# First attention: two accumulating transfers in place of two of TensorE's four sources of the denominators, with eight slots of probabilities

## The reference

```
cp = leaky_relu(x @ Wc.T + bc)                  # q, k: 16 heads x 8; v: 16 heads x 64
scores = einsum('bqhd,bkhd->bhqk', q, k) / SCALE
attn = softmax(scores, axis=-1)
out = einsum('bhqk,bkhd->bqhd', attn, v)
proj = leaky_relu(out @ Wo.T + bo)
```

## Time and profile before

| | us |
|---|---|
| median of the two runs | 1003.67 (1001.41 and 1005.93) |
| span of the profiled execution, first to last instruction | 1003.72 |
| first matmul of the denominators of unit 0, of unit 31 | 177.65, 612.77 |
| PE busy in the span | 920.3 (92%) |
| POOL busy in the span | 597.9 (60%) |

### The profile page before, as it was taken

The page is one execution under the profiler, slowest core; times in us unless marked ns, Lnnn a source line. Parts: engine busy times, 40 slices in busy tenths (PEclk is TensorE's granted clock), DMA queues, the critical chain, the costliest instruction groups (busy, mean ns, idle before and its releaser), DMA issues. The chain is left out here.

```text
span 1003.7 us, 20954 instructions
## 1 busy us (share of the span) xinstructions
PE 920.3 (92%) x7704; PEld 489.4 (49%) x7713; DVE 764.0 (76%) x1332; ACT 538.3 (54%) x901; POOL 597.9 (60%) x533
## 2 busy tenths in 40 slices
PE   5799997999999999999989997899889787799997
PEld 3346563233333333333323233798788444488794
DVE  6978888888888889887888825883689998873514
ACT  1255345666766666666756775443266243274463
POOL 3660425788778777887777893123735886652333
PEclk9999998999999999999999999799999997999999
DMA  9372525111111101111101123567651200243462
GB/s 319 137 225 88 153 64 156 41 51 46 26 52 28 58 24 49 34 55 56 35 26 44 40 67 116 161 193 241 225 156 35 89 22 22 79 142 101 143 196 79
DMA packets 92308, 97.17 MB, mean 97 GB/s; under 512 B 23184, under 2 KB 68624, under 8 KB 91952
## 3 DMA queue, kind: packets, MB, share of 16 engines
q1 hardware_dynamic: 87088, 85.34, 27.8%
q0 software_dynamic: 5120, 10.50, 3.6%
HBM read 70.57 MB, written 24.77 MB: 95 GB/s over the span
## 5 line engine op out<-in xcount | busy, mean ns | idle before, releaser
L255 PE MATMUL ps<-ar 64*64 64x512 bf16 (+5 forms) x5312 | 538.6, 448 | 17.7 <-ACT ar L301 4.3
L255 PEld LDWEIGHTS ps<-ar 64*64 64x64 bf16 (+2 forms) x5312 | 268.5, 137 | 273.4 <-ACT ar L301 92.0
L277 DVE TENSOR_REDUCE small<-ps 128x2 f32<-128x1024 f32 (+2 forms) x276 | 307.2, 1140 | 52.0 <-PE ps L255 50.6
L301 ACT ACTIVATE ar<-ps 128x1024 f32<-128x1024 f32 (+1 forms) x304 | 285.4, 941 | 113.1 <-PE ps L255 106.5
L264 POOL TENSOR_TENSOR psum_sb<-psum_sb,ar 128x1024 f32<-128x1024 f32 x91 | 214.8, 2360 | 57.3 <-DVE on_sb L264 47.1
L264 POOL TENSOR_TENSOR ar<-ar 128x512 f32<-128x512 f32 (+1 forms) x80 | 79.2, 995 | 52.1 <-DVE ar L277 30.0
L323 POOL DMA_INDIRECT gT<-ysort,rt x48 | 46.9, 977 | 98.7 <-issue 97.7
L264 DVE TENSOR_TENSOR ar<-ps,ar 128x256 f32<-128x256 f32 (+4 forms) x56 | 56.2, 1011 | 47.9 <-PE ps L255 43.4
L264 POOL TENSOR_TENSOR psum_sb<-ar 128x1024 f32<-128x1024 f32 x32 | 75.9, 2372 | 16.8 <-ACT ar L301 15.6
L298 ACT COPY ar<-ps 128x256 f32<-128x256 f32 (+1 forms) x84 | 31.8, 386 | 80.8 <-PE ps L255 50.2
L255 PE MATMUL ps<-wA,xnT 128*128 128x512 f32 (+3 forms) x192 | 62.0, 447 | 5.3 <-DVE ar L264 2.7
(11 more groups left out here) (156 smaller groups left out, 1066.0 us busy)
## 6 DMA issues: line engine op xcount, KB each, us to landing
ar<-in_L_up SPq DMA_DIRECT2D x48, 384.0 KB, 4.1
ar<-in_L_b SPq DMA_DIRECT2D x32, 322.0 KB, 3.4
rec_sb<-lscr SPq DMA_DIRECT2D x64, 128.0 KB
scr<-ar SPq DMA_DIRECT2D x48, 128.0 KB, 2.1
ar<-xsort SPq DMA_DIRECT2D x40, 128.0 KB
ysort<-ar SPq DMA_DIRECT2D x40, 128.0 KB, 3.3
ar<-scr SPq DMA_DIRECT2D x32, 112.0 KB
xsort<-xs SPq DMA_DIRECT2D x12, 256.0 KB, 6.2
```

What stands on the lines that cost most here:

```text
L255: return self.e.matmul(o, l, r, start=start, stop=stop) if self.e else Nothing()
L277: return self.e.tensor_reduce(o, a, AX.X, op, negate=True) if negate else self.e.tensor_reduce(o, a, AX.X, op)
L301: return self.e.activation(o, a, fn, **kw) if self.e else Nothing()
```

## The change

For the units with `u % 16 < 14` (`by_dma`, 28 of 32) POOL adds blocks 0 to 3 with three operations as before. Block 4 is added to that sum by an accumulating transfer that POOL issues at k = 6, and block 5 is added to block 6 in place by a second one at k = 7, issued after P times V of block 6 is done. At k = 1 of the next unit, behind that unit's first add, POOL waits for both transfers and adds block 6 (which now holds 5 and 6) to the sum. TensorE sums two sources, this sum and block 7, at k = 5 of the next unit (`SUM_STEP`) in place of k = 1. The steps of the reciprocal and of scaling move by four with it (k = 9, 10 and 14); the projection stays at k = 17 and takes a pair of banks of its own. There are eight slots, one for each block of a unit: two lie outside the old area (`ps2_sb`, and the new `p7_sb`). A slot's next `exp` waits for whatever reads it last (for block 5 the second transfer, for block 6 POOL's fourth add). POOL's wait for "scaled" is gone. `BY_DVE` goes from 27 to 30, so units 27 to 29 are done like the others; units 14, 15, 30 and 31 keep the four sources.

```diff
-BY_DVE = 27
-NP = 6
+BY_DVE = 30
+NP = 8
+SUM_STEP = 5
...
+    def dma_add(self, o, i):
+        return self.e.dma_start(o, i, accum_op=ALU.add) if self.e else Nothing()
...
+    p7_sb = sb("p7_sb", [128, 1024])
+    Ps = [area(POFF + 1024 * i, 1024) for i in range(6)] + [ps2_sb[:, :], p7_sb[:, :]]
...
+    def by_dma(u):
+        return u % 16 < 14
+    def sum_step(u):
+        return SUM_STEP if by_dma(u) else 1
...
-            if k == 1:
+            if k == sum_step(u) and by_dma(u):
+                b = island(u) + 1
+                pe.wait_ge(*at("exp", 8 * u + 7))
+                pe.wait_ge(*at("sums", u, 4))
+                for n, src in enumerate((Ps[7], psum_sb[:, 1024 * (u % 2):1024 * (u % 2) + 1024])):
+                    for a in range(2):
+                        r = 64 * n + 32 * a
+                        ins = pe.mm(ps[r:r + 32, b, :], onesf[:, 0:32], src[:, 512 * a:512 * a + 512])
+                ins.then_inc(*filled(b, ("sum", u)))
+            elif k == sum_step(u):
...
-                b = island(u + 2) if proj_step(u) == 17 else take(ring[0])
+                b = island(u + 2) if u % 16 in (12, 13) else take(ring[0])
...
+                    if by_dma(u) and k > 3:
+                        act.wait_ge(*(at("fourth_in", u), at("fifth_in", u), at("sums", u, 4), at("sum", u))[k - 4])
...
-                    if u >= BY_DVE:
-                        pool.wait_ge(*at("scaled", u - 2))
-                    pool.tt(a_, Ps[:, (i - 1) % NP, :], Ps[:, i % NP, :], ALU.add).then_inc(*up(("sums", u, 1)))
-                elif 2 <= k <= (4 if u < BY_DVE else 3):
-                    if k == 2 and 2 <= u < BY_DVE:
-                        pool.wait_ge(*at("scaled", u - 2))
+                    pool.tt(a_, Ps[0], Ps[1], ALU.add).then_inc(*up(("sums", u, 1)))
+                    if u and by_dma(u - 1):
+                        before = psum_sb[:, 1024 * ((u - 1) % 2):1024 * ((u - 1) % 2) + 1024]
+                        pool.wait_ge(*at("fourth_in", u - 1))
+                        pool.wait_ge(*at("fifth_in", u - 1))
+                        pool.tt(before, before, Ps[6], ALU.add).then_inc(*up(("sums", u - 1, 4)))
+                elif 2 <= k <= (3 if by_dma(u) or u >= BY_DVE else 4):
                     pool.wait_ge(*at("exp", i))
                     pool.wait_ge(*at("sums", u, k - 1))
-                    pool.tt(a_, a_, Ps[:, i % NP, :], ALU.add).then_inc(*up(("sums", u, k)))
+                    pool.tt(a_, a_, Ps[k], ALU.add).then_inc(*up(("sums", u, k)))
+                elif k == 6 and by_dma(u):
+                    pool.wait_ge(*at("exp", 8 * u + 4))
+                    pool.wait_ge(*at("sums", u, 3))
+                    pool.dma_add(a_, Ps[4]).then_inc(*landed(("fourth_in", u)))
+                elif k == 7 and by_dma(u):
+                    pool.wait_ge(*at("pvd", 8 * u + 6))
+                    pool.dma_add(Ps[6], Ps[5]).then_inc(*landed(("fifth_in", u)))
```

More of the change, by code:

```diff
@@ L509, in _program @@
     POFF = KOFF + 3 * 1024
-    assert POFF + NP * 1024 <= AR
+    assert POFF + 6 * 1024 <= AR
     V0 = area(0, 16384)
@@ L513, in _program @@
     Ks = area(KOFF, 3 * 1024).bitcast(BF16).rearrange("p (s h t) -> p s h t", s=3, h=2)
-    Ps = area(POFF, NP * 1024).rearrange("p (s t) -> p s t", s=NP)
     acc_sb = sb("acc_sb", [128, T])
@@ L789, in pv @@
                                 V0[r, 1024 * tile + 64 * h:1024 * tile + 64 * h + 64],
-                                Ps[r, i % NP, 512 * a:512 * a + 512], start=kt == 0, stop=kt == 7)
+                                Ps[i % NP][r, 512 * a:512 * a + 512], start=kt == 0, stop=kt == 7)
                 if kt == 7:
@@ L803, in unit_tail @@
                 pe.wait_ge(*(at("sums", u, 4) if u < BY_DVE else at("sums_dve", u)))
-                for n, src in enumerate((Ps[:, (8 * u + 5) % NP, :],
-                                         psum_sb[:, 1024 * (u % 2):1024 * (u % 2) + 1024],
-                                         Ps[:, (8 * u + 6) % NP, :], Ps[:, (8 * u + 7) % NP, :])):
+                for n, src in enumerate((Ps[5], psum_sb[:, 1024 * (u % 2):1024 * (u % 2) + 1024], Ps[6], Ps[7])):
                     for a in range(2):
@@ L1263, in unit_tail @@
                     *emptied(("pvd", 8 * u + 7), ("osb", u)))
-            if k == 5:
+            if k == sum_step(u) + 4:
                 dve.wait_ge(*at("lcol_in", u))
@@ L1270, in unit_tail @@
                 dve.rec(lsum, lsum).then_inc(*up(("lcol_dve", u)))
-            if k == 10:
+            if k == sum_step(u) + 9:
                 dve.wait_ge(*at(f"recip_in{m}", u))
@@ L1310, in attention @@
                     dve.wait_ge(*at("sums", u, 3))
-                    dve.tt(a_, a_, Ps[:, (8 * u + 4) % NP, :], ALU.add).then_inc(*up(("sums_dve", u)))
+                    dve.tt(a_, a_, Ps[4], ALU.add).then_inc(*up(("sums_dve", u)))
                 tails(i)
@@ L1858, in unit_tail @@
                     *emptied(("pvd_low", 8 * u + 7), ("osb_low", u)))
+            if k == sum_step(u):
                 act.wait_ge(*at("sum", u))
@@ L1878, in attention @@
                     k, u = (i - NP) % 8, (i - NP) // 8
-                    act.wait_ge(*(at("sum", u) if k > 4 else at("sums_dve", u) if k == 4 and u >= BY_DVE else
-                                  at("sums", u, max(k, 1))))
-                act.af(Ps[:, i % NP, :], ps[:, b0:b0 + 2, :].rearrange("p a t -> p (a t)"), ACT.Exp,
+                    if by_dma(u) and k > 3:
+                        act.wait_ge(*(at("fourth_in", u), at("fifth_in", u), at("sums", u, 4), at("sum", u))[k - 4])
+                    else:
+                        act.wait_ge(*(at("sum", u) if k > 4 else at("sums_dve", u) if k == 4 and u >= BY_DVE else
+                                      at("sums", u, max(k, 1))))
+                act.af(Ps[i % NP], ps[:, b0:b0 + 2, :].rearrange("p a t -> p (a t)"), ACT.Exp,
                        scale=SCALE).then_inc(*emptied(("st", i), ("exp", i)))
@@ L2367, in unit_tail @@
                 sp.dma(lcol[:, 8:16], lrow[64:128:32, :]).then_inc(*landed(("lcol_in", u)))
-            if k != 6:
+            if k != sum_step(u) + 5:
                 return
```

## The result

The changed kernel takes 1112.43 us (1111.48 to 1113.38) against 1003.67 us: a ratio of 1.108, interval 1.103 to 1.113. It is slower, as forecast, by 109 us where 58 were forecast; the time lies 2 us above the range.

A forecast was written before the change was run, and what follows sets the result against it. TensorE was taken to bound the attention before, POOL's turn after. To 1003.7 us came 39 us for turns 1.4 us longer in 28 units and 19 of side work: 1062 us, range 980 to 1110.

The forecast's parts named there:

- POOL's turn with a visible landing: POOL's queue per unit: two issues, W, three adds, 9.61 + W = 15.1 us against 13.71; chance 0.50, 1062 us.
- W: Time from the end of POOL's second issue to the landing, taken as 5.5 us, between 2.4 and 12.
- the second read and the queue: Half a microsecond added to the 5.0 us of a plain 512 KB transfer for reading the destination and queueing.
- The fourth rival: The second transfer waits for the first, two full reads each: landing 10.0 us, turn 19.6, 1188 us; chance 0.10.
- The lower end of my forecast: The forecast case by itself ran from 1025 us (landing after 4.1 us) to 1110 us (after 7.2 us).
- the lock: DVE's scaling stands still during a POOL add: 1.23 in place of 0.68 us in the one scaling that met one.
- the side work: POOL's gathers, scatters, normalisation and routing, 36 us from 200 to 600 us; half hidden, 19 us added to the time.
- Edits that I cost at nothing: Eight slots, moved steps, one more bank pair and units 27 to 29 were taken to add no time.
- the first rival: TensorE stays the bound, landing under 3.2 us: each unit gives 0.86 us, 980 us; chance 0.10.
- a floor: TensorE's two saved rounds, 0.86 us in 28 units, 24 us, all on the path: 1003.7 - 24 = 980 us.
- The third rival: Without POOL's wait for the scaled product, DVE's scaling meets POOL's adds and DVE becomes the bound: 1014 us; chance 0.08.
- its two signs: Signs that DVE had become the bound: DVE idle nowhere, and its scaling at 1.2 to 3 us.

The follow-up runs named there:

- the two-source run: The kernel before, with only TensorE's sum cut to the collected blocks and block 7 (blocks 5 and 6 left out of the denominators): 979.9 us, -21.

## Why the prediction was right, and where it was wrong

**The mechanism and the sign were right, and the sum was 50 us short.** POOL's turn with a visible landing sets the unit: POOL waits in nearly every unit, TensorE's sum waits up to 4.1 us for `psum_sb`, and taking the wait and its add away gives 78 of the 109 us back.

**The step that failed by size is W,** the time from the end of the second issue to its landing. I took 5.5 us; the landing of 7.6 less the issue of 1.10 makes 6.5, and 8.2 in the turn shown. The half microsecond for "the second read and the queue" was the error: plain copies in pairs land in 5.4 us, adding makes it 7.6, and alone an adding transfer takes 4.9. The Trainium skill ("Collectives: The Full Stack", section "The bandwidth ceiling: the fold count and why AG ≠ RS ≠ AR") has the two reads as the price of an add in the DMA engine, in collectives. The trace agrees that the add in flight has a price, 2.2 us for two transfers and 1.9 times the engines' time a megabyte; that it is the read and not the addition no run here shows. The fourth rival had the queueing right and its size (10 us) too large. With 6.5 my own sum gives 9.61 + 6.5 = 16.1, 28 x 2.4 = 67, and 1090 us. The lower end of my forecast holds a slip besides: W = 4.1 makes 1023 us by the same sum, not 1025.

**A wait was left out.** POOL's second issue waits for the product of block 6: 9.4 us over 22 units, 0.43 a unit, 12 us. I had named what queues behind the wait for the landing, but put the one in front of the issue at nothing. It is not made by TensorE's wait for POOL: with the sum at step 7, where that wait is gone, it is 11.5 us. With it the sum is 1102; the lock, some 10 us, brings it to 1112. That this meets the measured time to the microsecond is luck, as the next terms show.

**The other terms held, or cancelled.** The issues cost 0.91 and 1.10 us (0.97 and 1.27 taken) and the three adds 7.1 (7.37 taken), 0.5 us a unit less than I had; the gap ahead of the first issue (nothing taken) and the side work came 0.7 over. The mean unit between the sums of units 1 and 13 is (417.54 - 208.61) / 12 = 17.4 us: 2.0 of issues, 0.4 before the second, 6.5 of W, 7.1 of adds, 0.4 ahead of the first issue, and the 1.0 left over as side work (0.7 taken).

**"Edits that I cost at nothing" failed, unseen in the total.** The moved steps cost 24 us, as much as TensorE was to save; eight slots some 4 at most. I take both to lie under POOL's longer turn in the changed kernel; no run took them out of it. But they decide the first rival: with landings for nothing it would have come to about 1014 us, not 980, so my 0.10 for a faster kernel rested on a floor that this change couldn't reach. The PE saving itself, 0.86 us a unit, would be 27.5 us in the 32 units of the two-source run and measured 21.

**The third rival was priced too low by itself and mattered little here.** Alone the missing wait costs 48 us where I gave 10: I set the longer scaling against DVE's mean slack. In the changed kernel DVE idles anyway, and only some 10 us show. One of its two signs did show, the scaling at 2.4 us; the other, a DVE idle nowhere, did not (307.6 of 400 us busy). The Trainium skill ("SBUF — State Buffer", section "Who interferes with whom") has the rule that such a scaling and POOL's add shut each other out for a whole instruction. The trace agrees, with 2.4 us, the length of an add, in place of 0.68.

**A cost that stood nowhere in my sum** is the transfers' presence on the DMA engines: 25 us between half and whole transfers. The rows show small loads that come late (7.9 us of TensorE's waits) and the clock that falls behind the stall (6 us at 0.53 behind one of them); how the 25 us divide between these and other waits was not measured. How much of it lies in the 109 us is open too.

## What to carry to other kernels

A transfer that takes over an add moves its latency to the head of the queue that awaits it, and to the life of its source and destination slots: follow the loop (issue, landing, add, the next write into the slot, its use, the next issue) before the saved work is counted. Price steps that move by a run that undoes the rest of the change: here the reordering alone ate the whole saving. Slack counts only where it stands in the unit, so take a wait away only with the price of what it kept apart.

## What the runs showed that I had not expected

- An accumulating transfer of 512 KB within SBUF lands in 4.9 us alone and 7.6 behind another; 256 KB ones land in 3.5 and 4.4. POOL spends 0.9 to 1.1 us on each issue.
- The same matmuls take TensorE 12.99 in place of 12.60 us a unit when sum and projection stand apart, with no wait in either; each change between 64x64 and 128x32 tiles shows as 0.1 us.
- A stall of 2.8 us in TensorE was followed by 6 us at a granted clock of 0.53; the 2.8 us of a late 6 KB load thus cost about as much again (an estimate: 6 us at 0.53 do the work of 3.2 at full clock).
